# Second layers of two feed-forward blocks as three fp16 products, their inputs split by POOL and VectorE

## The chip, the cores and the metric

One core of a Trainium2 chip runs the whole program in one launch. The metric is the device time of the kernel in microseconds (us), the median of several executions. PE is TensorE, DVE is VectorE, ACT is ScalarE, POOL is GpSimd, SP is the queue that issues the DMAs.

## What is computed

32 independent batch items of 256 tokens by 256 features go through four stages. The two marked lines are what the change is about; the rest sets the work around them.

```
# per item: x is (256, 256), all in float32
x = x + W_out(silu(scale * LN2(W_in(silu(scale * LN1(x) + shift))) + shift))   # stage 0, norm over all 65536 values
x = ada(LN(x))                                                            # stage 1
x = x + Wo(softmax(q k^T / 4 + bias, masked) v)                           # 16 heads, bias (16, 256, 256) an item
x = x + gelu2(LN(x) @ W1 + b1) @ W2 + b2         # <- W1 (256, 1024), W2 (1024, 256)
x = max(x + dt * stencil(x), 0)                                           # stage 2
y = x + Wo3(causal attention(LN(x)))                                      # stage 3
y = y + gelu(LN(y) @ W3 + b3) @ W4 + b4          # <- W3 (256, 1024), W4 (1024, 256)
out = x + gate * (y - x)
```

## The kernel before

An item's activations are tiles of 128 partitions by 512 columns (two blocks of 256). All five instruction streams are written out by one loop over ticks: `begin(layer, b)` is 64 b for the first block of work (stages 0, 1 and 2) and 64 b + 160 for the last (stage 3), and the table `P` (with `OWN` for the first two and last two items, and `SPLIT`) gives each piece of work its tick from there. A tick is no time: it only fixes the order in which each engine's instructions stand, and each engine goes through its own list in that order, held by semaphores. So about three items are under way at once, and a piece that waits holds up all that stands behind it on its engine. Within a tick the order is that of the code: attention first, then the front, the middle, the stencil, the tail.

Attention is done in 16 units per item (8 for each block, two heads each), one every 4 ticks: scores on PE (L1538), bias and row maximum on DVE (L1010), exp on ACT (L1249), transposes on PE (L1548) and their copies from PSUM by ACT and DVE (L1254, L1017), the product with the values on PE (L1563). POOL adds the mask to the bias tile of each unit of the first block (L579), four tiles ahead at most, and makes the lower halves of q and k (L564, L567).

The feed-forward block of stage 1: `t2` transposes the normalized tile into bank `bM` (L1514), ACT writes it as fp16 to `hi(MB)` (`t2_out`, L1342), DVE writes what is missing as fp16 to `lo(MB)` (`t2_lo`, L949). `MB` is the tile `TN`, which stage 3 uses in the same way (`t4_out`, L1373). `widen` (L1447) makes the first layer in four quarters g of 256 hidden features, three fp16 products for each float32 one (upper x upper, upper x lower, lower x upper), from weights that were split into fp16 halves and scaled at the start (`WS`, from raw weights in `BB`: `split_scale`, `split_gains`, `split_rest` on DVE with L879, L888, L920, `split_high` on ACT, L1300). ACT adds the bias and writes the quarter to `AA[g]` (L1275), and four gelus turn `AA[0..3]` in place (L1351, after a table load). `narrow` (L1525) multiplies `AA[g]` with `W2` in float32 from `Wf` and sums the quarters in `bM`; `f1` adds the result to `X` (L1116), and the stencil follows (L1133 on DVE, L622 to L631 on POOL). Stage 3 does the same with `BB`, `bT_` and `W4` (L1264 gelu, `out` L1192).

Around them POOL has the root of the norms (`m1_rstd`: L554 to L559), and `m1_b`, which adds the bias `b21` to `X`. DVE's `all_center` (L969) reads two tiles of SBUF. At the start PE runs matmuls with no use of their result between the steps of the conditioning (`WARM`, L1397).

## Time and profile before

| | us |
|---|---|
| median of three runs | 2604.91 (2603.47 to 2608.86) |
| the profiled execution | 2604.97 |
| its span, first to last instruction | 2603.7 |
| one period in the middle (1482.10 to 1557.67) | 75.57 |

The profile is of one execution. "Busy" is the union of an engine's instructions in time; for PE the ends are modelled, as its products are pipelined. A group's row has the engine, the line, the tiles (written <- read) with shapes, the count, the busy time and the mean duration. A float32 product on PE stands as two records. The weight loads of PE (PEld) overlap with its products. A DVE or POOL instruction's duration includes any time in which it had been started and was held.

### The profile page before, as it was taken

What the parts mean: (1) busy time and instruction counts of PE and PEld (TensorE: products, weight loads), DVE (VectorE), ACT (ScalarE), POOL (GpSimd) and SP (SyncE); (2) the same over time, 40 slices, a digit from 0 to 9 for tenths busy, and PEclk for the clock granted to TensorE, in tenths of its full rate; (3) what the DMA queues carried; (4) which work ended last, traced back from release to release, by engine and by line L of the source; (5) the groups of instructions that cost most, each with busy time, mean ns of one, the idle gap of its engine ahead of it and who ended that gap; (6) DMA issues with size and microseconds to landing.
All of it is one profiled execution on the core that took longest, in us unless ns stands there. A gap on an engine that the chain in (4) does not pass through costs nothing.

```text
span 2603.7 us, 57961 instructions
## 1 busy us (share of the span) xinstructions
PE 2470.5 (95%) x19148; PEld 2005.6 (77%) x19148; DVE 2043.6 (78%) x7387; ACT 2115.3 (81%) x4694; POOL 1536.1 (59%) x1487
## 2 busy tenths in 40 slices
PE   6878999999999999999999999999999999999987
PEld 5666778778877877887887788778878877877776
DVE  6787878788888778888787888878888888878653
ACT  2466888888898888889888888988888888888875
POOL 2566666556666656666665656666556576655421
PEclk6899999999999999999999999999999999999999
DMA  5433443333344333334443333444433344433211
GB/s 205 120 119 105 121 127 113 111 106 106 107 122 126 112 110 108 107 105 122 126 115 108 108 107 106 122 127 115 114 110 100 105 121 125 123 105 96 75 29 33
DMA packets 178537, 287.67 MB, mean 110 GB/s; under 512 B 46080, under 2 KB 99328, under 8 KB 177984
## 3 DMA queue, kind: packets, MB, share of 16 engines
q1 hardware_dynamic: 178240, 283.97, 38.5%
q8 instruction: 155, 2.54, 0.4%
q14 instruction: 142, 1.16, 0.2%
HBM read 174.64 MB, written 8.45 MB: 70 GB/s over the span
## 4 chain that ended last, share of the span: by engine, by line
PE 69%; DVE 15%; SPq 4%; ACT 4%; issue 3%; POOL 2%; DMA 2%; DVEq 0%; POOLq 0%; ACTq 0%
PE bank L1525 17%; PE bank L1447 12%; PE bank L1548 10%; PE bank L1538 6%; PE bank L1563 6%; PE bank L1507 6%; DVE PB L1010 4%; PE bank L1514 3%; SPq L496 3%; PE bank L1459 3%; PE bank L1701 2%; DVE bank L969 2%; PE bank L1436 2%; SPq L492 1%; DMA Ks<-KU 1%
## 5 line engine op out<-in xcount | busy, mean ns | idle before, releaser
L1249 ACT ACTIVATE PB<-PB,mx 128x256 f32<-128x256 f32 (+1 forms) x2048 | 831.4, 473 | 35.7 <-DVE mx L1010 34.7
L579 POOL TENSOR_TENSOR BT<-BT,MN 128x1024 f32<-128x1024 f32 x256 | 556.9, 2180 | 122.5 <-DMA BT<-in_bias 121.0
L1548 PE MATMUL bank<-ident,PB 128*128 128x128 f32 x3584 | 486.4, 274 | 11.5 <-ACT PT L1254 5.5
L1010 DVE CUSTOM_DVE_ANT_0 PB<-bank,BT 128x256 f32<-128x256 f32 x1024 | 372.0, 418 | 137.8 <-PE bank L1538 132.8
L1548 PEld LDWEIGHTS bank<-ident,PB 128*128 128x128 f32 x3584 | 421.6, 141 | 63.4 <-ACT PB L1249 10.6
L1447 PE MATMUL bank<-TN,WS_w 128*128 128x256 f16 x3072 | 378.8, 273 | 38.7 <-ACT BB L1275 19.6
L1538 PE MATMUL bank<-Ks,Qs 96*128 96x512 f32 (+1 forms) x1024 | 364.6, 430 | 25.5 <-DMA Ks<-KU 12.0
L1017 DVE COPY PT<-bank 128x512 f32<-128x512 f32 (+1 forms) x512 | 315.9, 617 | 87.5 <-PE bank L1548 85.8
L1447 PEld LDWEIGHTS bank<-TN,WS_w 128*128 128x128 f16 x3072 | 282.5, 98 | 120.1 <-ACT BB L1275 35.4
L1254 ACT ACTIVATE PT<-bank 128x512 f32<-128x512 f32 (+1 forms) x512 | 272.3, 532 | 94.9 <-PE bank L1548 90.6
L1010 DVE CUSTOM_DVE_ANT_0 PB<-bank,caus 128x128 f32<-128x128 f32 (+1 forms) x1024 | 306.6, 350 | 42.3 <-PE bank L1538 42.2
L1563 PE MATMUL bank<-PT,VW 128*32 128x256 f32 (+1 forms) x4096 | 248.2, 360 | 4.4 <-DVE CX L1027 2.4
L1525 PE MATMUL bank<-Wf,BB 128*128 128x256 f32 x1024 | 236.8, 379 | 0.8 <-ACT BB L1264 0.6
L1525 PE MATMUL bank<-Wf,AA 128*128 128x256 f32 x1024 | 236.0, 383 | 0.5 <-ACT AA L1351 0.4
L1538 PEld LDWEIGHTS bank<-Ks,Qs 96*128 96x128 f32 x1024 | 168.1, 192 | 67.7 <-DVE mx L1010 22.3
L1525 PEld LDWEIGHTS bank<-Wf,AA 128*128 128x128 f32 x1024 | 192.2, 191 | 29.5 <-issue 0.9
L1525 PEld LDWEIGHTS bank<-Wf,BB 128*128 128x128 f32 x1024 | 189.6, 190 | 25.1 <-issue 1.7
L1563 PEld LDWEIGHTS bank<-PT,VW 128*32 128x32 f32 x4096 | 107.5, 109 | 98.7 <-issue 49.0
L554 POOL TENSOR_SCALAR smm<-smm 128x2 f32<-128x2 f32 x32 | 7.2, 226 | 280.0 <-DVE smm L991 280.0
L1010 DVE DVE_READ_ACCUMULATOR2_ANT mx<- 128x1 f32 x2048 | 169.0, 83 | 0.0
L1275 ACT ACTIVATE BB<-bank,cols 128x256 f32<-128x256 f32 x256 | 107.4, 470 | 44.3 <-PE bank L1447 44.3
L1260 ACT ACTIVATE ET<-bank 128x256 f32<-128x256 f32 x256 | 97.2, 380 | 46.8 <-PE bank L1563 42.7
(285 smaller groups left out, 4735.9 us busy)
## 6 DMA issues: line engine op xcount, KB each, us to landing
BT<-in_bias SPq DMA_DIRECT2D x256, 512.0 KB, 4.3
Qs<-QH SPq DMA_DIRECT2D x512, 64.0 KB, 2.4
Ks<-KH SPq DMA_DIRECT2D x1024, 32.0 KB, 2.0
Qs<-QU SPq DMA_DIRECT2D x256, 64.0 KB, 2.4
Ks<-KU SPq DMA_DIRECT2D x512, 32.0 KB, 2.0
XT<-in_xT SPq DMA_DIRECT2D x32, 256.0 KB, 2.8
X<-in_x SPq DMA_DIRECT2D x32, 256.0 KB, 2.9
AB<-ada_rows SPq DMA_DIRECT2D x32, 256.0 KB, 3.7
```

The source lines that it names most:

```text
L579: G.op.tensor_tensor(v2(BT[k % 4]), v2(BT[k % 4]), MN[:, :].unsqueeze(1).broadcast_to([128, 2, 512]), ALU.add).then_inc(g_bt, 1)
L1010: V.op.tensor_tensor_reduce(PB[(2 * D + q) % 6][:, h * 256:h * 256 + w], bS[q][:, h * w:h * w + w], plus, -1.0, 3.0e38, ALU.add, ALU.min, ...
L1017: V.op.tensor_copy(flipped(u.D, 1)[:, 0:w], bP[1][:, 0:w]).then_inc(v_ev, 1)
L1249: S.op.activation(o, o, ACT.Exp, scale=-1.0, bias=mx[u.layer][:, c:c + 1]).then_inc(a_exp, 1)
L1254: S.op.activation(flipped(u.D, 0)[:, 0:w], bP[0][:, 0:w], ACT.Copy).then_inc(a_ev, 1)
L1275: S.op.activation(half(out, m), half(ps, m), ACT.Identity, scale=scale(m), bias=bias(m)).then_inc(sem, 1)
L1447: last = T.op.matmul(half(ps, m), w, v[:, k * 256:k * 256 + 256], start=(k == 0 and i == 0), stop=(k == 1 and i == 2))
L1507: last = T.op.matmul(half(ps, m), x[:, k * 256 + m * 128:k * 256 + m * 128 + 128], Wf[:, a + k * 256:a + k * 256 + 256], start=(k == 0), s ...
L1525: last = T.op.matmul(half(ps, q), x[:, f * 256 + q * 128:f * 256 + q * 128 + 128], Wf[:, c:c + 256], start=(g == 0 and f == 0 and q == 0), ...
L1538: T.op.matmul(bS[q][:, 0:2 * w].rearrange("p (h k) -> p h k", h=2), Qs[i][0:96, et * 256 + q * 128:et * 256 + q * 128 + 128], k2[:, :, 0:w ...
L1548: last = T.op.transpose(bP[h][:, c * 128:c * 128 + 128], PB[(2 * u.D + q) % 6][:, h * 256 + k * 128:h * 256 + k * 128 + 128], ident[:, :])
L1563: last = T.op.matmul(half(bV, J % 2)[32 * s:32 * s + 32, q:256], VW[x][:, v:v + 32], flipped(u.D - 1 + et, h)[:, k * 256:k * 256 + 256 - q ...
```

## The change

Both `narrow`s take three fp16 products in place of a float32 one. `W2` and `W4` are loaded raw into `AA` and `BB` at the start, their maxima taken on DVE (`peek`), and split into fp16 halves (`narrow_high` on ACT, `narrow_rest` on DVE); `W4` is loaded twice, since `BB` holds `W3` in between. A bound for the hidden values gives one more scale, for which `split_gains` gets 19 more small operations in each block. In every item POOL writes the scaled upper half of each hidden quarter (`hidden_high`), and DVE the lower half in place (`hidden_rest`). The upper halves go to `TN` for g = 0 and 1 and to the free half of `AA[g-2]` or `BB[g-2]` for g = 2 and 3. `f1` and `out` undo the scale in the same instruction as their addition. All ticks are new: `w1_gelu` and `w2` from 64 and 68 to 62 and 70, `w3_gelu` and `w4` from 66 and 69 to 66 and 75, `f1` from 74 to 71.

```diff
+NARROW = {"w1": "w2", "w3": "w4"}
+HIDDEN = 32768.0
...
 WARM = {
-    "start": 24, "c1": 12, "n1_ones_0": 2, "v1": 9, "win_1": 5, "w1_0": 3, "n2_ones_2": 1, "n1_ones_3": 4,
-    "v1_3": 1, "v3": 10,
+    "start": 14, "c1": 13, "wout": 17, "v1": 11, "v3": 13,
...
+        def spare(x, b, g):
+            if x == 3 and b == NB - 1:
+                return (hi, lo)[g % 2](AA[g // 2])
+            return (hi, lo)[g](TN) if g < 2 else lo((AA if x == 1 else BB)[g - 2])
...
+                for b in at(t, "ld_w1"):
+                    if b == 0:
+                        S.wait_ge(p_set, 5)
+                        raw("w1", BB, d_ws)
+                        raw("w2", AA, d_wn)
...
+            def hidden_high(x, layer, b, g, sem):
+
+                G.op.tensor_scalar(spare(layer, b, g), x[:, :], narrow_scale("w2" if layer == 1 else "w4", 7), None,
+                                   ALU.mult).then_inc(sem, 1)
...
+                for b, g in steps(t, "h1_hi", 4, 1):
+                    G.wait_ge(a_h1, 4 * b + g + 1)
+                    G.wait_ge(v_ws, made("p3"))
+                    if g < 2:
+                        G.wait_ge(p_w1, 4 * b + 4)
+                    else:
+                        G.wait_ge(v_h1, 4 * b + g - 1)
+                    hidden_high(AA[g], 1, b, g, g_h1)
...
+            def peek(n):
+
+                for c in range(4):
+                    V.op.tensor_reduce(aq[:, c:c + 1], raw_narrow(n)[c][:, :], AX.X, ALU.max,
+                                       apply_absolute_value=True).then_inc(v_ws, 1)
+
+            def narrow_rest(n):
+
+                j = ("w2", "w4").index(n)
+                for c in range(4):
+                    z = 512 * c
+                    V.wait_ge(a_wn, 4 * j + c + 1)
+                    V.op.scalar_tensor_tensor(out=WS[n][:, 2048 + z:2560 + z], in0=raw_narrow(n)[c][:, :],
+                                              scalar=narrow_scale(n, 6), in1=WS[n][:, z:z + 512], op0=ALU.mult,
+                                              op1=ALU.subtract).then_inc(v_wn, 1)
...
+            def hidden_rest(x, layer, b, g, sem):
+
+                V.op.scalar_tensor_tensor(out=hi(x), in0=x[:, :], scalar=narrow_scale("w2" if layer == 1 else "w4", 7),
+                                          in1=spare(layer, b, g), op0=ALU.mult, op1=ALU.subtract).then_inc(sem, 1)
...
+                for b, g in steps(t, "h1_lo", 4, 1):
+                    V.wait_ge(g_h1, 4 * b + g + 1)
+                    hidden_rest(AA[g], 1, b, g, v_h1)
...
                     V.wait_ge(p_w2, 4 * b + 4)
                     V.wait_ge(g_m1, 5 * b + 5)
-                    V.op.tensor_tensor(x[:, :], bM[:, :], x[:, :], ALU.add).then_inc(v_f1, 1)
+                    V.op.scalar_tensor_tensor(out=x[:, :], in0=bM[:, :], scalar=narrow_scale("w2", 4), in1=x[:, :], op0=ALU.mult,
+                                              op1=ALU.add).then_inc(v_f1, 1)
...
                 for b in at(t, "t2_out"):
                     S.wait_ge(p_t2, b + 1)
-                    S.wait_ge(p_w3, 4 * (b - 2))
+                    S.wait_ge(p_w2, 4 * b)
+                    S.wait_ge(p_w4, 4 * (b - 2))
...
                 for b in at(t, "t4_out"):
                     S.wait_ge(p_t4, b + 1)
-                    S.wait_ge(p_w1, 4 * min(b + 3, NB))
+                    S.wait_ge(p_w2, 4 * min(b + 3, NB))
+                    S.wait_ge(p_w4, 4 * b)
...
-            def narrow(ps, x, w, g):
+            def narrow(ps, n, h, l, g):
                 for f in range(2):
                     for q in range(2):
-                        c = w * 2048 + (2 * g + f) * 256
-                        last = T.op.matmul(half(ps, q), x[:, f * 256 + q * 128:f * 256 + q * 128 + 128], Wf[:, c:c + 256],
-                                           start=(g == 0 and f == 0 and q == 0), stop=(g == 3 and f == 1),
-                                           skip_group_check=True)
+                        z, c = (2 * g + f) * 256, slice(f * 256 + q * 128, f * 256 + q * 128 + 128)
+                        wh, wl = WS[n][:, z:z + 256], WS[n][:, 2048 + z:2304 + z]
+                        for i, (v, w) in enumerate(((h, wh), (h, wl), (l, wh))):
+                            last = T.op.matmul(half(ps, q), v[:, c], w, start=(g == 0 and f == 0 and q == 0 and i == 0),
+                                               stop=(g == 3 and f == 1 and i == 2), skip_group_check=True)
...
                 for b, g in steps(t, "w2", 4, 1):
-                    T.wait_ge(d_w2, 16)
+                    T.wait_ge(v_wn, 4)
                     T.wait_ge(a_w1, 8 * b + 8)
-                    T.wait_ge(a_h1, 4 * b + g + 1)
-                    narrow(bM, AA[g], 0, g).then_inc(p_w2, 1)
+                    T.wait_ge(g_h1, 4 * b + g + 1)
+                    T.wait_ge(v_h1, 4 * b + g + 1)
+                    narrow(bM, "w2", spare(1, b, g), hi(AA[g]), g).then_inc(p_w2, 1)
```

Stage 3 has the same steps as `h3_hi`, `h3_lo` and `w4`, with `BB` for `AA`.

## Rows read from the trace of the kernel before

**Rows 1.** The page of before: its span, busy shares by engine, and PE's 40 slices.

```profile
span 2603.7 us, 57961 instructions
...
PE 2470.5 (95%) x19148; PEld 2005.6 (77%) x19148; DVE 2043.6 (78%) x7387; ACT 2115.3 (81%) x4694; POOL 1536.1 (59%) x1487
...
PE   6878999999999999999999999999999999999987
```

**Rows 2.** Table of stretches: us, then busy us (instructions) of each engine, PE's clock, DMA.

```profile
...
0.00:320.00 320.00, 258.57 (x1741) 204.43 (x1742) 244.40 (x799) 179.39 (x386) 171.94 (x162) 0.87 0.44 135
320.00:2240.00 1920.00, 1886.18 (x14886) 1539.63 (x14889) 1564.18 (x5707) 1660.09 (x3695) 1202.98 (x1164) 1.00 0.40 113
2240.00:2604.00 364.00, 325.74 (x2526) 261.56 (x2524) 235.03 (x883) 275.78 (x615) 161.23 (x162) 1.00 0.29 76
1482.10:1557.67 75.57, 74.37 (x590) 60.75 (x589) 61.66 (x228) 65.56 (x147) 47.95 (x47) 1.00 0.41 115
```

**Rows 3.** Groups of instructions on PE by form: shapes, count, busy us, mean ns, idle before.

```profile
...
L1447 PE MATMUL bank<-TN,WS_w 128*128 128x256 f16 x3072 | 378.8, 273 | 38.7 <-ACT BB L1275 19.6 <-ACT AA L1275 10.6 <-DVE TN L949 4.6
...
L1525 PE MATMUL bank<-Wf,BB 128*128 128x256 f32 x1024 | 236.8, 379 | 0.8 <-ACT BB L1264 0.6
L1525 PE MATMUL bank<-Wf,AA 128*128 128x256 f32 x1024 | 236.0, 383 | 0.5 <-ACT AA L1351 0.4
...
L1459 PE MATMUL bank<-WS_p,HB 128*128 128x256 f16 x384 | 48.0, 275 | 0.1
```

**Rows 4.** Timeline of the last 16 us: start, length, engine, line, count; PE's rows.

```profile
...
2587.75 5.40 PE L1447 MATMUL bank<-TN,WS_w 128*128 128x256 f16 x48
...
2592.99 7.07 PE L1525 MATMUL bank<-Wf,BB 128*128 128x256 f32 x32
```

**Rows 5.** Single lines: count, least/median/most ns, first and last start; L920's group has its mean.

```profile
L1116 DVE TENSOR_TENSOR X<-bank,X x32: 678/681/692, 158.5 to 2500.8; 128x512 f32<-128x512 f32 x32
...
L920 DVE SCALAR_TENSOR_TENSOR WS_w<-BB,ws,WS_w x8: 740/1271/2619, 76.2 to 187.0; 128x512 f16<-128x512 f32 x8
...
L1133 DVE TENSOR_TENSOR bank<-X,cB x32: 706/1404/1801, 159.7 to 2504.7; 128x512 f32<-128x512 f32 x32
...
L969 DVE SCALAR_TENSOR_TENSOR bank<-XT,sm,gT x64: 749/1759/2723, 19.0 to 2363.0; 128x512 f32<-128x512 f32 x64
...
L879 DVE TENSOR_REDUCE am<-BB x14: 407/664/681, 49.0 to 148.1; 128x1 f32<-128x512 f32 x8, 128x1 f32<-128x256 f32 x6
...
L888 DVE TENSOR_REDUCE am<-am x3: 157/157/158, 52.0 to 150.7; 128x1 f32<-128x4 f32 x2, 128x1 f32<-128x6 f32 x1
...
L920 DVE SCALAR_TENSOR_TENSOR WS_w<-BB,ws,WS_w 128x512 f16<-128x512 f32 x8 | 11.6, 1512 | 0.4 <-ACT WS_w L1300 0.4
```

**Rows 6.** Single lines of POOL: count, least/median/most ns, first and last start.

```profile
L564 POOL TENSOR_TENSOR QU<-QU,QH x64: 1267/1278/1586, 61.7 to 2536.6; 128x512 fp32r<-128x512 f32 x64
...
L573 POOL TENSOR_SCALAR MN<-MU x32: 1493/1494/1819, 73.2 to 2365.6; 128x512 bf16<-128x512 uint8 x32
...
L579 POOL TENSOR_TENSOR BT<-BT,MN x256: 2117/2138/2670, 74.8 to 2437.8; 128x1024 f32<-128x1024 f32 x128
```

**Rows 7.** Waits of DVE, then of POOL: us in total, times, longest.

```profile
...
DVE PB L1010 <- PE bank L1538: 175.0, 136, 4.3
...
POOL smm L554 <- DVE smm L991: 280.0, 32, 10.0
```

**Rows 8.** Timeline around one period: f1 and t4_out, then out.

```profile
1505.54 0.68 DVE L1116 TENSOR_TENSOR X<-bank,X 128x512 f32<-128x512 f32 x1
...
1521.11 0.60 ACT L1373 ACTIVATE TN<-bank 128x512 f16<-128x512 f32 x1 [0.23 <-PE bank L1514]
...
1544.63 0.70 DVE L1192 TENSOR_TENSOR bank<-bank,Y 128x512 f32<-128x512 f32 x1 [1.05 <-PE bank L1525]
```

**Rows 9.** Timeline of the last 16 us, ACT's first and last gelu.

```profile
...
2590.13 0.72 ACT L1264 ACTIVATE BB<-BB,ws 128x512 f32<-128x512 f32 x1
...
2594.58 0.72 ACT L1264 ACTIVATE BB<-BB,ws 128x512 f32<-128x512 f32 x1
```

More of the change, by code:

```diff
@@ L79 @@
     "v3_out", "c3", "c3_out", "o3", "m4", "m4_rstd", "m4_norm", "m4_b", "t4",
-    "t4_out", "w3", "w3_out", "w3_gelu", "w4", "out", "st_out",
[1 row of a table added]
 }
@@ L641, in gpsimd @@
                     token_rstd(smt, g_t, 6 * b, NORM)
+                for b, g in steps(t, "h3_hi", 4, 1):
+                    G.wait_ge(a_ge, 4 * b + g + 1)
+                    G.wait_ge(v_ws, made("w3") + 40)
+                    if b == NB - 1:
+                        G.wait_ge(v_s, 17 * NB)
+                    elif g < 2:
+                        G.wait_ge(p_w3, 4 * b + 4)
+                    else:
+                        G.wait_ge(v_h3, 4 * b + g - 1)
+                    hidden_high(BB[g], 3, b, g, g_h3)
                 for b in at(t, "m4_b"):
@@ new lines, in split_gains @@
+                high, wide_raw, bias, beta, wide_max, bound, up, down = (narrow_scale(NARROW[n], i) for i in (0, 1, 2, 3, 4, 5, 6, 7))
+                a = 8 * ("w1", "w3").index(n)
+                V.op.tensor_scalar(wn[:, a:a + 5], ps[:, 128:133], 128.0, None, ALU.mult).then_inc(v_ws, 1)
+                V.wait_ge(v_ws, v0 + 6)
+                V.op.tensor_tensor(bound, wide_raw, beta, ALU.mult).then_inc(v_ws, 1)
+                V.op.reciprocal(up, high).then_inc(v_ws, 1)
+                V.wait_ge(v_ws, v0 + 8)
@@ new lines, in split_gains @@
+                V.op.tensor_tensor(bound, bound, wide_max, ALU.add).then_inc(v_ws, 1)
+                V.op.tensor_scalar(up, up, LARGE, None, ALU.mult).then_inc(v_ws, 1)
+                V.wait_ge(v_ws, v0 + 10)
+                V.op.scalar_tensor_tensor(out=bound, in0=bound, scalar=256.0, in1=bias, op0=ALU.mult, op1=ALU.add).then_inc(v_ws, 1)
+                V.wait_ge(v_ws, v0 + 11)
+                V.op.reciprocal(down, bound).then_inc(v_ws, 1)
+                V.op.tensor_tensor(wide_max, bound, high, ALU.mult).then_inc(v_ws, 1)
@@ L913, in split_rest @@
                 first = sum(len(split_of(m)[1]) for m in ORDER[:ORDER.index(n)])
-                v0 = made(n) + len(parts) + 11
+                v0 = scaled(n)
                 ps = bM if n == "w1" else bT_
@@ L1187, in tail @@
                     token_stats(y, smt, v_t, 5 * b + 1)
+                for b, g in steps(t, "h3_lo", 4, 1):
+                    V.wait_ge(g_h3, 4 * b + g + 1)
+                    hidden_rest(BB[g], 3, b, g, v_h3)
                 for b in at(t, "out"):
@@ L1219, in vector @@
                         first_rest()
+                for b in at(t, "split_peek"):
+                    if b == 0:
+                        V.wait_ge(d_wn, 128)
+                        peek("w4")
+                for n in NARROW.values():
+                    for b in at(t, f"split_{n}_lo"):
+                        if b == 0:
+                            narrow_rest(n)
                 for n in ORDER:
@@ L1292, in project, with narrow_high @@
                         S.op.activation(f32r(hi), U[:, :], ACT.Copy).then_inc(a, 1)
+            def narrow_high(n):
+                S.wait_ge(v_ws, scaled("w1" if n == "w2" else "w3"))
+                if n == "w4":
+                    S.wait_ge(d_wn, 192)
+                for c in range(4):
+                    S.op.activation(WS[n][:, 512 * c:512 * c + 512], raw_narrow(n)[c][:, :], ACT.Identity,
+                                    scale=narrow_scale(n, 6)).then_inc(a_wn, 1)
             def split_high(n):
-                k0 = made(n) + len(split_of(n)[1]) + 11
+                k0 = scaled(n)
                 S.wait_ge(v_ws, k0)
@@ L1747, in tensor @@
                         T.wait_ge(v_o, 2 * b)
-                    T.wait_ge(d_w4, 16)
-                    T.wait_ge(a_ge, 4 * b + g + 1)
-                    narrow(bT_, BB[g], 1, g).then_inc(p_w4, 1)
+                    T.wait_ge(v_wn, 8)
+                    T.wait_ge(g_h3, 4 * b + g + 1)
+                    T.wait_ge(v_h3, 4 * b + g + 1)
+                    narrow(bT_, "w4", spare(3, b, g), hi(BB[g]), g).then_inc(p_w4, 1)
         loads()
```

175 lines of the change are left out of this document (118 added, 57 removed), and 148 rows, old and new, of tables (LATE, OWN, P).

## The prediction

> **What bounds the kernel now.** I read the page's shares and its slices first [rows 1]: TensorE (PE) is busy 95% of a span of 2603.7 us, and all its slices in the middle are full at full clock, while VectorE (DVE) stands at 78%, ScalarE (ACT) at 81% and POOL at 59%. The table of stretches [rows 2] shows where the rest lies. From 320 to 2240 us PE is busy 1886.2 of 1920 (98.2%); in the first 320 us only 258.6, and in the last 364 us 325.7, for there the chains of single batch items, not the amount of work, set the pace. One period, from the first layer's `t2_out` of one item at 1482.10 to the next one's at 1557.67, is 75.57 us. In it PE is busy 74.37, DVE 61.66, ACT 65.56, POOL 47.95. So in the middle the bound is PE's work, with 1.2 us of waits per item. DVE's own largest wait is for PE's scores, 175.0 us in all [rows 7]; it has 13.9 us of slack per item, POOL has 27.6. The middle holds 1920 / 75.57 = 25.4 of the 32 items; 6.6 items' worth lies in the ends.
>
> **What leaves PE.** `narrow` (L1525) is the second layer of both blocks. It runs in fp32, in which each product leaves two records; 1024 records for each block, 236.0 and 236.8 us busy [rows 3]. After the change each product is three fp16 ones: 2 blocks x 32 items x 4 quarters x 4 products x 3 = 3072, each 128x128 against 256 columns. This form is in the trace: L1447, 3072 records in 378.8 us; and L1459, where the weights are the moving side as they will be here, 384 in 48.0 us, so 125 ns each [rows 3]. By busy time the trade is 472.8 - 384 = 89 us. Busy spans of small groups overlap their neighbours', so I prefer distances between starts. In the tail 48 fp16 products start at 2587.75 and what follows starts at 2592.99: 5.24 us, 1.31 for the 12 that will make a quarter. The 32 fp32 records then run 7.07 us, 1.77 for the 8 that make a quarter now [rows 4]. The saving is 0.45 us a quarter, 3.6 us an item, 115 us in all (bounds 89 to 115). I take 0.45. With the same 1.2 us of waits PE's period would be 75.57 - 3.6 = 71.97 us. The startup's warm matmuls change a little (68 instead of 71): nothing.
>
> **What DVE gets.** Eight `hidden_rest` per item, SCALAR_TENSOR_TENSOR over 128x512, both tensor inputs in SBUF, fp16 out (256 in all). The same form stands in the trace as L920 (the weights' lower halves): least 740, median 1271, most 2619 ns; its mean, 1512, has the startup's few in it [rows 5]. The least is what the work takes; DVE ops of the same size with one input in PSUM hold 678 to 692 (L1116) and never more. The others with two inputs in SBUF stretch: L1133 706 to 1801, median 1404, where POOL runs its `s_pm`, and L969 749 to 2723, median 1759 [rows 5]. So the surplus is a wait inside the instruction while POOL is in one of its own (1.28 us for 512 elements, 2.14 for a mask addition [rows 6]). The Trainium skill, "SBUF — State Buffer", section "SBUF: two separate sides", gives the cause: a DVE instruction with two SBUF inputs and a POOL instruction exclude each other for their whole length. By that rule these 256 belong to the stretching kind, and the trace agrees (the page names no cost; the medians above do). What matters is how often POOL is in an instruction when a `hidden_rest` comes up. `hidden_high(g+1)` stands in POOL's order right behind `hidden_high(g)`, whose end releases `hidden_rest(g)`: a clash is built in for g = 0 and 2. For g of 2 and 3 POOL itself waits for `hidden_rest(g-2)`, which keeps it quiet at other moments. About half blocked: I take L920's median, 1.27 us; bounds 0.74 and 1.76. DVE per item: 61.66 + 8 x 1.27 = 71.8 us (67.6 to 75.7). `f1` and `out` stay single instructions with one input in PSUM: nothing.
>
> So DVE comes level with PE. DVE can't be busy all the time: it takes turns with PE through the same banks (scores, transposes). PE alone runs now at 98.4%; two engines that are both nearly full wait for each other more. I give DVE 97.5% at best: 71.8 / 0.975 = 73.6 us a period, against PE's 71.97. 73.6 is the forecast for the middle: 1.97 us an item less, 25.4 items: -50 us. The bounds: with unblocked halves DVE needs 67.6 / 0.975 = 69.3, PE decides, 3.6 us an item: -91. With 1.76 us each: 75.7 / 0.975 = 77.6, +2.0 an item: +52.
>
> **What POOL gets.** Eight `hidden_high` per item, TENSOR_SCALAR 128x512, fp32 to fp16. Nearest rows: 1.28 us for a two-input addition of that size, 1.49 for a TENSOR_SCALAR from uint8 [rows 6]. I take 1.28: 47.95 + 10.2 = 58.2 of 73.6 us, 79%; up to 3 us more where DVE holds it off. It doesn't bound, and costs nothing by itself. The Trainium skill, "GPSIMD Engine Reference", section 3, puts a tight one-input loop over 512 elements at 769 ns; by it POOL would need 6.2 us an item, block DVE for less, and the forecast would go toward the lower bound; no row here shows such an instruction. The first half waits for ACT's gelu, and behind it in POOL's order stand mask additions, `m1_b` and the stencil's first products. POOL now sits waiting for DVE 280.0 us in `m1_rstd` alone [rows 7], 8.75 an item, and four bias tiles lie between a mask addition and its user, so this is covered; were it not, the scores' biasing on DVE would be late by up to one chain of four gelus of 0.72 us [rows 9], 2.9 us in each block.
>
> **The longer way from gelu to the second layer.** Now `w2` starts behind the gelu; the change puts at least 1.28 + 0.74 us between, for four quarters up to 8.1. PE has other items' work in between if the order allows (the ticks part `w1_gelu` and `w2` by 8 instead of 4, 9 us), so I cost it at nothing. Uncovered it would be 2 to 8 us in each block.
>
> **TN is held longer.** TN holds the first layer's input halves, then the hidden halves of quarters 0 and 1, for both blocks in turn. Now from `t2_out` at 1482.10, where the period of [rows 2] begins, to `f1` at 1505.54, when `w2` is over, are 23.4 us, and from `t4_out` at 1521.11 to `out` at 1544.63, when `w4` is over, 23.5 [rows 8]. The free parts are 15.6 and 13.0 us. Even 8.1 us more in each leaves 7.5 and 4.9. The new waits of `t2_out` and `t4_out` for `p_w2`, `p_w4` are covered.
>
> **Start.** Raw `w2` is loaded with `w1`; DVE gets four reductions of 0.66 us (L879), some 19 small operations of about 0.16 (L888), and four lower halves of 0.74 to 1.5: 9 to 12 us [rows 5]; ACT gets four copies, and has room. Part of it lies in the first item's chain, where PE is idle anyway. The same for `w4` one item later. I take +5; bounds 0 and +20.
>
> **The ends.** Outside the middle 6.6 items' work shrinks by 3.6 us each, 24 us, but PE isn't the limit there: I take half, -12 (bounds 0, -24). The very end: the last gelu starts at 2594.58 and the fp32 products then run to 2600.06 [rows 4, 9]; new, gelu's end at 2595.30 + 1.28 + 0.74 + 1.31 is 2598.6, or 2600.3 if the four quarters' halves alternate (from the first gelu's end at 2590.85, 8.1 + 1.31): 0.
>
> **Sum**, against the profiled execution (2604.97 us with a span of 2603.7; the median of the three runs is 2604.91, the same): 2604.97 - 50 - 12 + 5 = 2548 us.
>
> **Rivals.** (a) PE stays the bound, the halves slip in unblocked, 2604.97 - 91 - 24 + 5 = 2495. For it: POOL idles 27.6 us an item, and quiet stretches of 4 to 10 us could be met. Against: the built-in clash. (b) DVE becomes the bound for worse than PE was, slower than before. From a mean `hidden_rest` of (75.57 x 0.975 - 61.66) / 8 = 1.50 us on; L920's mean of 1.51 is there already, L969's median gives 2604.97 + 52 + 10 = 2667; at 1.65 us each the period is 76.8, +30 us, about 2640. Against: a late DVE meets a POOL that waits for it. (c) Level: period 75.0 to 75.6, the gain eaten by waits between PE and DVE, or by the gelu chain; 2590 to 2610. (d) The change doesn't do what it says: fp16 products cost more here, since each brings a weight load of its own. L1447 and L1459 load as often, at 123 to 125 ns [rows 3], so I give this almost nothing; the price is 89 instead of 115 us, 7 us later in a PE-bound case.
>
> **How the numbers follow.** The forecast, 2525 to 2580, has 0.48; between it and (a) 0.17, near (a) 0.05; (c) 0.12; a small gain from 2580 to 2595 0.06; (b) 0.12. The range 2495 to 2612 leaves out (b) and a little of (a), and takes the bounds of the unknown stretch of `hidden_rest` nearly whole. 0.2% is 5 us, about what a measurement can tell from no change. Faster by more than that: 0.79; within: 0.06; slower: 0.15.
>
> **What would show it.** Right: L1525's records are 3072 fp16 of some 125 ns; the period in the middle about 73.6; DVE busy over 90% in the middle, PE below 97% there, with waits for DVE that rows of before don't have; `hidden_rest` with a least of 0.74 and a median near 1.27. Wrong: a median at 0.74 to 0.9 (then (a)); PE waiting for `hidden_rest` itself (the gelu chain isn't covered); waits of `t2_out` or `t4_out` (TN); a startup later by over 10 us at the first `f1`.

## The result, and the profile after

The changed kernel takes 2837.07 us (median of 4 runs, 2832.17 to 2837.49), the kernel before 2605.12 beside it: ratio 1.0884, 95% interval 1.0868 to 1.0900. It is slower by 232 us; the prediction said 57 us faster. The page of the changed kernel, its first part and two of its slices' rows, against [rows 1]:

```profile
span 2835.9 us, 60959 instructions
## 1 busy us (share of the span) xinstructions
PE 2456.8 (87%) x20148; PEld 1928.3 (68%) x20148; DVE 2352.1 (83%) x7689; ACT 2114.6 (75%) x4702; POOL 1981.1 (70%) x1743
...
PE   6677888988898898888888988888998889988887
...
PEclk7879999999999999999999999999999999999999
```

No engine is full any more. Most of PE's slices of 9 have become 8s, and it is not the clock that took them away: the granted clock is still 9 (tenths of full speed) in every slice from the fourth on, and 0.99 on average in the middle. The stretches, columns as in [rows 2]:

```profile
320.00:2240.00 1920.00, 1710.84 (x14408) 1350.61 (x14407) 1649.96 (x5417) 1519.54 (x3395) 1436.59 (x1255) 0.99 0.36 104
```

PE is busy 89% of the middle (98.2% in [rows 2]), DVE 86%, ACT 79%, POOL 75%. The period comes most exactly from `f1`, one instruction an item (name, form, count, ns least/median/greatest, first and last start):

```profile
L1244 DVE SCALAR_TENSOR_TENSOR X<-bank,wn,X x32: 743/747/752, 172.2 to 2729.1; 128x512 f32<-128x512 f32 x32
```

(2729.1 - 172.2) / 31 = 82.48 us. Before, the same instruction (L1116) started at 158.5 first and at 2500.8 last: 75.56 us. All periods below are worked out so. The whole loss can be placed with it: the first `f1` is 13.7 us later, 31 periods are 6.92 us longer each (214.6), and from the last `f1` to the span's end it is 106.8 us instead of 102.9. Sum 232.2, the difference of the two spans. The loss is in the repeated part.

What each engine is busy per item is its share of the middle times 82.48: PE 73.5, DVE 70.9, ACT 65.3, POOL 61.7. The two kinds of new instruction, DVE's `hidden_rest` and POOL's `hidden_high`, by tile (ns least/median/greatest):

```profile
L1069 DVE SCALAR_TENSOR_TENSOR AA<-AA,wn,TN x64: 743/1173/2643, 160.4 to 2722.6; 128x512 f16<-128x512 f32 x64
L1069 DVE SCALAR_TENSOR_TENSOR BB<-BB,wn,TN x62: 743/748/1181, 371.4 to 2809.8; 128x512 f16<-128x512 f32 x62
...
L593 POOL TENSOR_SCALAR TN<-AA,wn x64: 1561/1572/1860, 157.0 to 2720.9; 128x512 f16<-128x512 f32 x64
```

And waits of PE, of DVE and of POOL (engine, line waited at, releaser: us in all, times, longest). Those at L1692, L1069 and L593 are new; PE's wait for DVE's maxima was 10.6 us before, and POOL's for the bias tile 121.0:

```profile
PE bank L1704 <- DVE mx L1135: 66.2, 99, 4.2
PE bank L1692 <- DVE AA L1069: 49.3, 58, 3.7
...
DVE AA L1069 <- POOL TN L593: 83.4, 57, 2.7
...
DVE PB L1135 <- PE bank L1704: 44.3, 57, 3.6
...
POOL TN L593 <- ACT BB L1405: 167.4, 30, 29.5
POOL BT L623 <- DMA BT<-in_bias: 141.8, 36, 8.6
...
POOL TN L593 <- ACT AA L1506: 25.6, 22, 12.8
```

The new ones, read from the bottom up, are the steps of one path: gelu (ACT) to `hidden_high` (POOL) to `hidden_rest` (DVE) to the product (PE, L1692). PE and DVE wait at it for the block with `AA`; for `BB` PE's wait for the lower half is 3.6 us in all, and it is POOL that stands early, waiting for the gelu. DVE's wait for PE's scores, 175.0 us in [rows 7], has shrunk to 44.3; PE now waits for DVE's maxima, 66.2. The two changed places. How POOL's list stands in it is seen in its timeline, with ACT's gelus of the second block last (start, us, what, idle time before it and what ended it):

```profile
1510.85 1.28 POOL L689 TENSOR_TENSOR Y<-X,rows 128x512 f32<-128x512 f32 x1
1518.45 3.12 POOL L593 TENSOR_SCALAR TN<-BB,wn 128x512 f16<-128x512 f32 x2 [6.32 <-ACT BB L1405]
...
1553.13 2.13 POOL L623 TENSOR_TENSOR BT<-BT,MN 128x1024 f32<-128x1024 f32 x1 [5.04 <-DMA BT<-in_bias]
1555.28 1.57 POOL L593 TENSOR_SCALAR TN<-AA,wn 128x512 f16<-128x512 f32 x1
...
1554.46 2.56 ACT L1506 ACTIVATE AA<-AA,ws 128x512 f32<-128x512 f32 x4
```

POOL stands 6.32 us before the halves of one block, waiting for their gelu. Before the halves of the other block it stands 5.04 us for a bias tile and then adds the mask. It looks as if that made the halves late, but it did not: their first gelu started at 1554.46 and took 0.71 us, so its result was there at 1555.17, and POOL began 0.11 us later. The timeline of the whole run shows the same. In 29 of the 32 items the first half of `AA` starts within 0.2 us of the first gelu's end, and that of `BB` always. POOL begins on time; what it adds to the path is what the halves, and the small steps between them, take.

### The profile page after: what moved, and what is told of

The parts are those of the page before. It is cut to its first block, busy times and chain, and to the rows that moved or that the text cites. A ratio compares the mean times of both kernels' runs of the same rounds, so it can differ in the third digit from the quotient of the medians.

```text
span 2835.9 us, 60959 instructions
## 1 busy us (share of the span) xinstructions
PE 2456.8 (87%) x20148; PEld 1928.3 (68%) x20148; DVE 2352.1 (83%) x7689; ACT 2114.6 (75%) x4702; POOL 1981.1 (70%) x1743
## 4 chain that ended last, share of the span: by engine, by line
POOL 27%; DVE 24%; PE 22%; ACT 12%; issue 10%; SPq 2%; DMA 1%; DVEq 0%; POOLq 0%; ACTq 0%
POOL TN L593 6%; POOL BT L623 6%; PE bank L1604 6%; DVE PB L1135 5%; PE bank L1692 3%; PE bank L1714 3%; ACT PB L1390 2%; PE bank L1672 2%; ACT AA L1416 2%; PE bank L1679 2%; PE bank L1729 2%; POOL AA L593 2%; PE bank L1704 2%; DVE PT L1142 2%; DVE BB L1069 2%
## 5 line engine op out<-in xcount | busy, mean ns | idle before, releaser
L623 POOL TENSOR_TENSOR BT<-BT,MN 128x1024 f32<-128x1024 f32 x256 | 571.3, 2242 | 141.9 <-DMA BT<-in_bias 141.8
L1714 PE MATMUL bank<-ident,PB 128*128 128x128 f32 x3584 | 564.1, 277 | 17.2 <-DVE PT L1142 11.5
L1714 PEld LDWEIGHTS bank<-ident,PB 128*128 128x128 f32 x3584 | 445.5, 143 | 97.2 <-ACT PB L1390 22.1
L1704 PE MATMUL bank<-Ks,Qs 96*128 96x512 f32 (+1 forms) x1024 | 425.0, 449 | 88.8 <-DVE mx L1135 66.2
L593 POOL TENSOR_SCALAR TN<-BB,wn 128x512 f16<-128x512 f32 x62 | 96.9, 1570 | 167.4 <-ACT BB L1405 167.4
L1692 PE MATMUL bank<-WS_w,AA 128*128 128x256 f16 x1056 | 170.9, 274 | 36.3 <-DVE AA L1069 27.0
L1692 PE MATMUL bank<-WS_w,TN 128*128 128x256 f16 x1008 | 176.9, 278 | 24.9 <-DVE AA L1069 22.3
L1692 PE MATMUL bank<-WS_w,BB 128*128 128x256 f16 x1008 | 162.9, 273 | 2.8 <-DVE BB L1069 1.6
L1416 ACT ACTIVATE AA<-bank,cols 128x256 f32<-128x256 f32 x256 | 107.4, 470 | 50.3 <-PE bank L1604 49.6
L1692 PEld LDWEIGHTS bank<-WS_w,AA 128*128 128x128 f16 x1056 | 99.8, 98 | 60.8 <-issue 34.8
```

The lines of the kernel that those rows point to most:

```text
L593: G.op.tensor_scalar(spare(layer, b, g), x[:, :], narrow_scale("w2" if layer == 1 else "w4", 7), None, ALU.mult).then_inc(sem, 1)
L623: G.op.tensor_tensor(v2(BT[k % 4]), v2(BT[k % 4]), MN[:, :].unsqueeze(1).broadcast_to([128, 2, 512]), ALU.add).then_inc(g_bt, 1)
L1416: S.op.activation(half(out, m), half(ps, m), ACT.Identity, scale=scale(m), bias=bias(m)).then_inc(sem, 1)
L1692: last = T.op.matmul(half(ps, q), v[:, c], w, start=(g == 0 and f == 0 and q == 0 and i == 0), stop=(g == 3 and f == 1 and i == 2), skip_g ...
L1704: T.op.matmul(bS[q][:, 0:2 * w].rearrange("p (h k) -> p h k", h=2), Qs[i][0:96, et * 256 + q * 128:et * 256 + q * 128 + 128], k2[:, :, 0:w ...
L1714: last = T.op.transpose(bP[h][:, c * 128:c * 128 + 128], PB[(2 * u.D + q) % 6][:, h * 256 + k * 128:h * 256 + k * 128 + 128], ident[:, :])
```

## The experiments

Five parts of the change can be had one by one: the start, the shorter products, the new order, the hand-overs of the halves, and the time that the halves take. The first four runs (a single execution each; the kernel before gave 2602.84 on the same chip) keep the new order and take parts of the halves away.

**New order, fp32 products, no halves.** The `hidden_high` and `hidden_rest` steps are gone, and the products are the old ones; they read columns of `Wf` that hold other weights, in the same form and number.

```diff
-                        for i, (v, w) in enumerate(((h, wh), (h, wl), (l, wh))):
-                            last = T.op.matmul(half(ps, q), v[:, c], w, ...
+                        last = T.op.matmul(half(ps, q), h[:, f * 256 + q * 128:f * 256 + q * 128 + 128], Wf[:, z:z + 256],
```

> The changed kernel with all its new ticks and its startup, but the second layers in float32 as before (from tiles AA and BB, against float32 weights of another layer, so the values differ) and no hidden halves on POOL and DVE. It is the old work in the new order. If the new order costs the time (theory ORDER), at least 2750 us. If the halves cost it (theories POOL or DVE), within 2600 to 2640: the startup's 14 us and little else.

2781.61 us, period 80.63. The new order and the new start, with the work of before in the middle, cost 5.1 us an item. This was the first sign of the step that failed.

**New order, fp16 products, no halves.** The products take weight tiles as operands.

```diff
-                    narrow(bM, "w2", spare(1, b, g), hi(AA[g]), g).then_inc(p_w2, 1)
+                    narrow(bM, "w2", WS["w2"][:, 0:512], WS["w2"][:, 512:1024], g).then_inc(p_w2, 1)
```

> The changed kernel without the hidden halves on POOL and DVE; the fp16 products read weights in their place and wait for the gelus alone. It shows what PE's saving is worth where nothing is added: by my forecast's term 3.6 us an item less than the run in float32 where PE bounds (about -115 us against it); theory ORDER: as slow as the float32 one, since PE isn't the bound there.

2672.25 us, period 77.2: the shorter products give 109 us, 3.4 us an item (forecast: 3.6 and 115). In this order the saving comes through nearly whole.

**One half at a time.** First POOL's halves whole and DVE's of 2 columns; then DVE's whole and POOL's of 2 columns. The products read weight tiles where a half is missing.

```diff
-                V.op.scalar_tensor_tensor(out=hi(x), in0=x[:, :], ...
+                V.op.scalar_tensor_tensor(out=hi(x)[:, 0:2], in0=x[:, 0:2], ...
```

> POOL makes the whole upper halves, DVE only two columns of each lower half; PE reads weights as the lower halves. All waits stand. Theory POOL (the halves stand in the middle of POOL's order and hold up what is behind them): at least 2780 us. Theory DVE (1.17 us instructions with the lock take DVE's slack): 2650 us or less.

```diff
-                G.op.tensor_scalar(spare(layer, b, g), x[:, :], ...
+                G.op.tensor_scalar(spare(layer, b, g)[:, 0:2], x[:, 0:2], ...
```

> The other way round: POOL writes two columns of each upper half, DVE the whole lower halves; all waits stand. Theory DVE: at least 2780 us. Theory POOL: 2650 us or less. If both single ones lie near 2740, each adds its part to one common chain.

2782.07 and 2786.54 us. Either half alone costs 110 to 114 us over the run without halves, both together 165. The price of POOL's part, which the forecast put at nothing, is as large as that of DVE's. Two loads on two independent bounds would leave the larger one; two links of one chain would add up. They seem to lie between, but both runs contain all the hand-overs, and a later run prices these.

**The old order with room for the halves.** The obvious question is whether the old ticks would have been better. They can't be kept as they are, since TensorE would wait at `w2` for halves that come later in the lists of engines that wait for TensorE. So `w2` goes from 68 to 70, `w4` from 69 to 73, `out` from 74 to 76, `st_out` from 71 to 73. The rest stays, but for a few ticks of the start and of the first and last two items.

```diff
-    "w2": 68, "w4": 69, "out": 74, "st_out": 71,
+    "w2": 70, "w4": 73, "out": 76, "st_out": 73, "h1_hi": 58, "h1_lo": 66, "h3_hi": 54, "h3_lo": 70,
```

> The whole change (fp16 products, both halves, the new startup) with the old kernel's ticks for all that existed before; the new pieces are put in by hand (POOL's upper halves at 58 and 54, DVE's lower halves at 66 and 70, w2 at 70, w4 at 73, out at 76, and a few ticks of the last two items). My forecast of 2548 us was for a kernel with the old order's waits. Theory ORDER AND HALVES (the new order costs 5 us an item by itself, the halves 5 more, whatever the order): 2837 - 179 = about 2660 us. If my sum was right and only the order was missed: 2530 to 2580. If the halves need the new order: above 2700.

3649.39 us, ratio 1.4004 (1.3975 to 1.4034). The same ticks with fp16 products and no halves, with POOL's halves alone and with DVE's alone:

> The fp16 products in the old order, without the hidden halves (weights are read in their place): PE's saving in the order in which PE was the bound. By the forecast's term 3.6 us an item: 75.6 - 3.6 = 72.0 us a period, 2604.97 - 115 + 5 = about 2495 us. If the saving is as in the new order (109 us), the same within 10.

> As old_order, but DVE writes only two columns of each lower half and PE reads weights for them: POOL's share of the cost in the old order. Theory POOL: as slow as old_order within 30 us. Theory DVE: near old_f16_none.

> As old_order, but POOL writes only two columns of each upper half (DVE subtracts weights in their place, and PE reads the same weights): DVE's share in the old order. Theory DVE: as slow as old_order within 30 us. Theory POOL: near old_f16_none. If both are slow, the chain gelu, POOL, DVE, PE and its waits cost, not the work of one engine.

2908.56, 3572.7 and 3513.08 us, a single execution each. `old_f16_none` missed its expectation by over 400 us, and `old_high_only` both of its cases (it lies 77 us below `old_order`). For `old_order` and `old_rest_only` only the last case of each held, that the halves need the new order and that the chain costs and not the work of one engine; neither had named a price near the 900 to 1040 us above the kernel before. Waits of `old_order`, the whole change in this order, for PE, DVE and POOL, and its middle stretch:

```profile
PE bank L1574 <- POOL X L544: 247.4, 29, 10.6
PE bank L1587 <- DVE AA L964: 213.7, 30, 9.7
...
DVE AA L964 <- POOL TN L488: 256.2, 37, 15.6
...
POOL AA L569 <- DVE X L1139: 259.3, 31, 13.5
...
320.00:2240.00 1920.00, 1413.09 (x10804) 1089.07 (x10802) 1197.16 (x4052) 1151.54 (x2544) 1069.10 (x942) 0.85 0.27 78
```

I read them as a ring: PE waits at `w2` (L1587) for DVE's half, DVE for POOL's half, POOL in the stencil for DVE's `f1` (L1139), which needs `w2`, and the next block's halves stand behind that in POOL's list. Each of these waits is 7 to 8.4 us an item, the period is 107.6, and no engine is over 74% busy. For the halves the new order is thus 812 us better than this one, and it is no waste by itself. But even the run without halves, at 2908.56, is 303 us slower than the kernel before, from which it differs in a few ticks, the shorter products and the start. Hence the next runs.

**Moved ticks by themselves.** The kernel before, complete, with only these ticks later (and `w2` of the first and last two items by one or two):

```diff
-    "w2": 68, "w4": 69, "out": 74, "st_out": 71,
+    "w2": 70, "w4": 73, "out": 76, "st_out": 73,
```

> The kernel before, complete and with fp32 second layers; only the ticks of w2 (68 to 70), w4 (69 to 73), out (74 to 76) and st_out (71 to 73) are later. Theory that a piece moved by a few ticks in TensorE's list is what costs: 2800 to 3000. Rival, that the cost comes with the shortened fp16 products or the reordered start: 2600 to 2640, as before.

2947.78 us, ratio 1.1323 (1.1302 to 1.1345), period 86.3: the theory holds. Moving a few matmuls that PE has to do anyway two to four ticks back costs more than the change under study. DVE's `f1` and `out` in that run, each with its idle time:

```profile
L1021 DVE TENSOR_TENSOR X<-bank,X x32: 685/692/693, 157.0 to 2833.5; 128x512 f32<-128x512 f32 x32
its engine sat idle before it (us, times) until:
  PE bank L1430: 129.6, 30
...
L1097 DVE TENSOR_TENSOR bank<-bank,Y x32: 689/700/700, 347.6 to 2939.2; 128x512 f32<-128x512 f32 x32
its engine sat idle before it (us, times) until:
  PE bank L1430: 129.1, 31
```

In the kernel before the same instruction idled once:

```profile
L1116 DVE TENSOR_TENSOR X<-bank,X x32: 678/681/692, 158.5 to 2500.8; 128x512 f32<-128x512 f32 x32
its engine sat idle before it (us, times) until:
  PE bank L1525: 1.0, 1
```

Now DVE stands 8.3 us an item with the scores of the next heads behind it, and PE needs those. Two runs ask how this price behaves. One tick instead of two to four:

```diff
-    "w2": 68, "w4": 69, "out": 74, "st_out": 71,
+    "w2": 69, "w4": 70, "out": 75, "st_out": 72,
```

> The kernel before, complete, with the second layers and what reads them one tick later: w2 68 to 69, w4 69 to 70, out 74 to 75, st_out 71 to 72; f1 stays at 74. A tick is 75.6/64 = 1.2 us here. Moved by two and four ticks, f1 and out stood 8.6 us an item for TensorE and the period rose by 10.8 us. If the price begins where the slack between w2 and f1 (six ticks, 7 us) is used up: 2610 to 2680. If any move costs as much as the large one, because the neighbours in TensorE's list change: 2850 to 2950. No price: 2600 to 2610.

2675.83 us, ratio 1.0272 (1.0249 to 1.0295), period 77.7, 32.3 us of standing at `f1`. It begins at the first tick, with +71 us (68 against the kernel before on the same chip), and grows with the distance. PE's wait for ACT's copy of the transposed probabilities is 31.5 us there, 5.5 in the kernel before, and for DVE's maxima 31.3 against 10.6. And the readers moved along, so that `f1` and `out` stand as far behind the products as in the kernel before (the edit is against the run with ticks moved by two to four):

```diff
-    "f1": 74, "s_r": 75, "out": 76, "st_out": 73,
+    "f1": 76, "s_r": 77, "out": 78, "st_out": 75,
```

> The kernel before with w2, w4 and out late as in the run that moved these alone (86.3 us a period), and now f1 (74 to 76), s_r and a further two ticks of out (to 78) and st_out (to 75) later as well. In that run VectorE stood 4.3 us an item at f1 and 4.3 us at out, behind TensorE. If those 8.6 us of standing were the price of the move, most of the 343 us goes: 2620 to 2720. If the price lies in TensorE's own list: 2850 to 2950.

3050.2 us, ratio 1.1708, period 89.7. Neither expectation has it: it grew by 102 us, though the standing at `f1` is gone:

```profile
L1021 DVE TENSOR_TENSOR X<-bank,X x32: 678/685/691, 163.8 to 2944.3; 128x512 f32<-128x512 f32 x32
its engine sat idle before it (us, times) until:
  PE bank L1430: 6.4, 3
...
DVE PB L915 <- PE bank L1443: 303.2, 136, 10.4
...
POOL AA L527 <- DVE X L1021: 220.8, 31, 8.8
```

The wait went to others: POOL's stencil now stands 220.8 us for `f1` (140.6 with only the products moved, 21.2 in the kernel before), DVE 303.2 for scores (192.7, and 175.0 in [rows 7]). Part of the price is not waiting at all. PE's busy time an item is 74.2 us in the kernel before, 77.0 with the products moved and 78.7 here, for the same matmuls, at a granted clock of 1.00, 0.98 and 0.95 in the middle. So my account of that price by DVE's standing alone is refuted; which of PE's neighbours costs what in these lists stays open.

**The old order to the tick.** Without halves the old ticks can be kept, all but those of the loads and the new steps of the start and four of the last two items. Two runs, first with fp16 products on weight tiles, then with the fp32 products of the first experiment; both with the change's start.

```diff
-    "w1_gelu": 62, "w2": 70, "f1": 71, "w4": 75, "out": 76, ...
+    "w1_gelu": 64, "w2": 68, "f1": 74, "w4": 69, "out": 74, ...
```

> Leaves out: both halves of the hidden values (the three fp16 products read weight tiles in their place), so the output is not the reference's. The order is the old one to the tick: w2 at 68, w4 at 69, out at 74. If the saving on TensorE is real and only the order stood in its way, the time falls by the term of the forecast, 89 to 115 us and some us of start: 2490 to 2530. If moving w2 and w4 by two to four ticks was not what made the run with shifted ticks 300 us slower, it stays near that one, 2850 to 2910.

> Complete, second layers in fp32 and no halves, the old order to the tick; what is left of the change is its start (the narrow weights' halves are made before the first items). It prices the start by itself. The run with fp16 products in this order was 2584 with the first f1 at 179.8 us against 158.5 before. Expected: the period of before, 75.6 us, and a start 15 to 25 us longer, 2618 to 2632; so that TensorE's shorter products gave 35 to 45 us in this order. Rival, a start that is covered later: 2600 to 2610.

2584.45 us (ratio 0.9924, 0.9909 to 0.9939) and 2639.64 (1.0129, 1.0107 to 1.0151). Each lies above its expected range, the first by 54 us, the second by 8. The second is not complete, contrary to its expectation, but reads other columns of `Wf`, like the first experiment. Periods 74.23 and 75.90. The start and what comes with it cost 33 us against the kernel before on the same chip: the first `f1` is at 173.8 us instead of 158.5 (15), 31 periods are 0.34 us longer each (11), and from the last `f1` to the end it is 7 us more. The shorter products give 55 us here, 1.67 an item, not the 3.6 of the forecast. The middles of the fp32 and of the fp16 run:

```profile
320.00:2240.00 1920.00, 1886.07 (x14894) 1536.96 (x14893) 1566.12 (x5710) 1659.43 (x3698) 1209.42 (x1166) 1.00 0.39 113
...
320.00:2240.00 1920.00, 1851.94 (x16064) 1499.60 (x16062) 1599.72 (x5839) 1694.14 (x3783) 1230.73 (x1191) 1.00 0.40 116
```

PE's busy time an item falls from 74.6 (1886.07 / 1920 x 75.90) to 71.6 us, but its gaps grow from 1.3 to 2.6. They lie in the attention: PE's wait for ACT's copy of the transposed probabilities is 30.4 us in all (5.5 in the kernel before), for DVE's maxima 21.9 (10.6). My reading, which no run tests, is that scores, bias and maximum, exponential, transposes and copies go round PE, DVE and ACT, and that `w2` and `w4` were filler that gave the other two time.

**More work off PE, no halves.** If fewer products are the point, the halves can be dropped: the gelu writes fp16, and two products remain (hidden values rounded to fp16, which the change avoids).

```diff
-                        for i, (v, w) in enumerate(((h, wh), (h, wl), (l, wh))):
+                        for i, (v, w) in enumerate(((h, wh), (h, wl))):
...
-                S.op.activation(BB[g][:, :], BB[g][:, :], ACT.Gelu, scale=scale_of("w3", 0)).then_inc(a_ge, 1)
+                S.op.activation(hi(BB[g]), BB[g][:, :], ACT.Gelu, scale=scale_of("w3", 0)).then_inc(a_ge, 1)
```

> Old order to the tick. The gelu writes its result as fp16 at once and the second layers are two fp16 products (hidden times high half, hidden times low half of the weight); POOL and VectorE make no halves. The hidden values are then rounded to fp16, which the kernel of the change does not do. Each quarter has 12 fp16 matmuls where the three products have 18 records' worth, so TensorE loses a further 0.4 us a quarter, 3 us an item. If the order lets the saving through: 2400 to 2460. If ScalarE (65.6 us of each 75.6 before) or another chain takes over early: 2460 to 2520. If TensorE is no longer the bound after the first 115 us, it equals the run with three products and no halves.

2596.21 us, ratio 0.9963 (0.9950 to 0.9975). This beats both kernels, by 9 us over the one before. But it has a third fewer fp16 products in the second layers than the fp16 run above and is 12 us slower. Of its expectation only the third case is near, that it equals that run. Its middle and PE's wait, from an execution of 2603.27 us, 7 above the median:

```profile
320.00:2240.00 1920.00, 1797.26 (x15138) 1423.49 (x15137) 1595.02 (x5801) 1684.89 (x3754) 1221.92 (x1183) 0.98 0.40 114
...
PE bank L1609 <- ACT PT L1290: 80.2, 35, 2.8
```

Period 74.68, PE busy 69.9 of it: 1.7 us less an item, and 2.1 us more gaps. The products taken away are worth more than 1.7 us. All second-layer products were busy 366.8 us in the run above and are 255.7 here, 3.5 us an item less. About half of that is eaten up inside PE's busy time, at a granted clock of 0.98 in the middle where the run above has 1.00: the transposes (280 ns in the mean against 275) and the products with the values (406 against 390) are longer. How much of the 12 us is the clock and how much the attention's waits no run separates. What is shown is that beyond the first 1.7 us of shorter period, work taken off PE bought nothing in this order.

**What of the halves costs.** The changed kernel with all its waits and signals, the halves of 2 columns on both engines, the products on weight tiles:

```diff
-                G.op.tensor_scalar(spare(layer, b, g), x[:, :], ...
+                G.op.tensor_scalar(spare(layer, b, g)[:, 0:2], x[:, 0:2], ...
...
-                V.op.scalar_tensor_tensor(out=hi(x), in0=x[:, :], ...
+                V.op.scalar_tensor_tensor(out=hi(x)[:, 0:2], in0=x[:, 0:2], ...
```

> Leaves out: POOL's and VectorE's instructions for the halves write 2 columns in place of 512, and the fp16 products read weight tiles; all waits and signals of the changed kernel stay, and so does its order. Without the halves this order gave a period of 77.2 us, with them 82.5. If it is their duration (1.57 us on POOL, 1.0 to 1.6 us on VectorE, 8 of each an item) that costs: 2675 to 2720. If it is the hand-overs gelu to POOL to VectorE to TensorE in queues that are worked in order: 2760 to 2837.

2709.12 us, ratio 1.0397 (1.0374 to 1.0420), period 78.5. The hand-overs cost 37 us (1.3 an item over 77.2), the duration of the halves 128 us (4.0 an item). That the hand-overs in ordered queues are the larger part is refuted, the more so as the short instructions are not free: POOL's take 0.29 us each, DVE's 0.48 in the mean. With these 37 us taken off, POOL's halves alone cost 73 us and DVE's alone 77. Their sum, 150, is not far above the 128 of both together: what the two engines spend on the halves nearly adds up, as in a chain.

**The mask addition.** In the changed kernel POOL's `mask_add` 4 ticks later, so that the halves don't stand behind it:

```diff
-    "mask_add": -25,
+    "mask_add": -21,
```

> The changed kernel, complete; only POOL's addition of the mask comes 4 ticks later (-25 to -21), so that fewer halves queue behind it while it waits for its bias tile (141.8 us of waiting, 36 times). If POOL's standing in front of the halves is on the chain that sets the period: 2740 to 2815. If not: 2825 to 2850. Worse than 2850 if the bias then comes late for the scores.

2923.77 us, ratio 1.1215 (1.1188 to 1.1243), period 85.2: the run went the third way that the expectation named. POOL's waiting for the bias tile fell from 141.8 to 24.9 us, and in its place came

```profile
DVE PB L1115 <- POOL BT L603: 75.9, 34, 4.1
...
POOL TN L573 <- ACT AA L1486: 174.6, 29, 12.8
```

DVE now stands for the masked bias (5.1 us before the move), and POOL waits for the gelu of `AA` instead of the bias tile (25.6 us before). The path through the halves gains nothing: PE waits 48.7 us for `hidden_rest` of `AA` (49.3 before), DVE 82.1 for POOL (83.4). That agrees with the timeline above, in which POOL wasn't late for the gelu.

## Why the prediction was wrong, step by step

The loss adds up over a row of runs, each a step from the one before it: start and the rest of the new frame +35 us (2604.9 to 2639.6), shorter products in the old order -55 (to 2584.5), the new order +88 (to 2672.3), hand-overs +37 (to 2709.1), duration of the halves +128 (to 2837.1). Sum +232. The run at 2672.3 is a single execution, and the runs stand on several chips, on which the kernel before had medians of 2602.8 to 2607.8. The division between the steps depends on their sequence: in the new order the shorter products give 109 and the order by itself costs 142 (2639.6 to 2781.6). The forecast failed at two terms that it put at nothing, the new order (88 to 142 us) and the way through the halves (37 + 128 = 165 us), and in one that it took whole, PE's saving (55 us came through in the old order, not 115).

- **The new ticks.** This is the step that failed first. The text has the ticks only as cover for the gelu's path, and gives their replacement no term and no rival. They cost 88 to 142 us at equal work. The trace of before had a sign: DVE's `f1` waited 1.0 us in all, with `w2` six ticks ahead of it. A table so exactly used up is itself a resource, and the change has to move `w2` away from `w1_gelu`. Which of the new ticks cost the 88 to 142 us is not shown: nearly all differ, and the runs that move single ones start from the old table.
- **"In the middle the bound is PE's work".** True as a reading, 98.2%, but wrong as the derivative. Of 3.0 us that leave PE in the old order 1.67 reach the period. The forecast took 1.2 us of waits as fixed; they doubled. This is what rival (c) says, a gain eaten by waits between PE and DVE or by the gelu chain; it has the right mechanism, but its 2590 to 2610 us is far short of 2837.
- **DVE.** The load was right: 70.9 us an item against 71.8. `hidden_rest` has a mean of 1.19 us (305.0 us in 256) against 1.27 taken, least 0.72 to 0.74, and stretches to 2.64 where POOL works beside it. But 97.5% as DVE's ceiling was not what held: it is 86% busy. Rival (b) has the right sign and the wrong mechanism; it asks for DVE at its ceiling. (Its sum 2604.97 + 52 + 10 = 2667 has 10 us for start and ends where the forecast has 5 and -12; the text doesn't say from where.)
- **POOL "doesn't bound, and costs nothing by itself".** `hidden_high` took 1.57 us, above the 1.28 taken and the 1.49 of the other row that the text names, and its half alone cost 110 us, 73 without the hand-overs. Its share of 75% says nothing about a link in a chain: 8 x 1.57 = 12.6 us an item lie between gelu and product. The Trainium skill, "GPSIMD Engine Reference", section 3, has 769 ns for a tight loop over 512 elements. The rows here show about twice that, 1.57 us; the measurement decides.
- **The longer way from gelu to the second layer,** put at 0, "uncovered it would be 2 to 8 us in each block". It was uncovered: PE waits 49.3 us for the `hidden_rest` of `AA` itself (1.5 us an item), and DVE 83.4 us for POOL's half (2.6). The text had named this as a mark of being wrong. It gave 2 to 8 us in each block, 4 to 16 an item; the halves with their hand-overs cost 5.3 us an item (82.48 - 77.20), inside that. The choice of 0 was the mistake.
- **PE's saving** was right in size: 3072 fp16 records, and 3.4 us an item where it came through. **TN** was right: no large wait of ACT stands for it (2.8 and 2.3 us in all).
- **Start** +5, bounds 0 and +20: the first `f1` came 13.7 us later, inside, though past the 10 us that the text names as a sign of being wrong. The whole new frame, with its small share in each period and at the end, cost 33 us in the old order, outside. **Ends** -12: measured +3.9 after the last `f1`, outside the bounds of that term.

## What to carry to other kernels

A share of 98% tells which engine to relieve, not what the relief is worth: ask what the second engine on the same loop does with less time, and expect the gain to stop early (here 1.7 of 3.0 us). In a kernel whose engines work hand-made lists in order, a changed order is a term of the sum: find the instructions that wait almost nothing for a producer placed closely ahead, and price every producer that the change has to push back. A new stage between two others costs its duration along the chain even on an engine that is a quarter idle and begins it on time. Before a wait in a timeline is blamed, look at when what stands behind it could have started.

## What the runs showed of the hardware

POOL's multiplication with a column from fp32 to fp16 over 128x512 took 1557 ns at the least and 1562 to 1572 in the median of each tile, in 256 executions, longer than its two-input addition of the same size (1.28 us).

`hidden_rest` stretched from 0.72 to 2.64 us. How it is held shows in the run with 2 columns on both engines. On the last two quarters of `AA` the 2-column instruction takes 1235 ns in the median, on the first two 218:

```profile
L1069 DVE SCALAR_TENSOR_TENSOR AA<-AA,wn,TN x64: 202/218/243, 161.4 to 2597.5; 128x2 f16<-128x2 f32 x64
L1069 DVE SCALAR_TENSOR_TENSOR AA<-AA,wn x64: 208/1235/2176, 162.4 to 2598.2; 128x2 f16<-128x2 f32 x64
...
1490.95 1.49 DVE L1069 SCALAR_TENSOR_TENSOR AA<-AA,wn 128x2 f16<-128x2 f32 x1
...
1490.29 2.13 POOL L623 TENSOR_TENSOR BT<-BT,MN 128x1024 f32<-128x1024 f32 x1
```

The instruction of DVE starts inside POOL's mask addition and ends 0.02 us after it, at 1492.44: what it takes is the rest of POOL's instruction, not its own work. The next one, at 1494.13, takes 1.23 us and ends 0.02 us after the POOL addition that was running then. POOL's halves can't be what holds it there, at 0.29 us each. In the whole kernel it is similar. With POOL's halves alone cut to 2 columns the mean of `hidden_rest` stayed: on `AA` 1.29 us against 1.32 (165.1 and 169.4 us in 128 each), on `BB` 1.04 against 1.06 (132.7 and 135.6 in 128 each), while the median on `AA` fell from 1173 to 773 ns. So the clash that the prediction saw built in between `hidden_high` and `hidden_rest` is not what sets the mean; with POOL's halves short, its other work, such as the mask addition above, holds DVE for as long. The clash exists all the same: with POOL's halves whole and DVE's of 2 columns, DVE's took 181.2 us in all, against 123.5 with both short.

In `old_order` PE was busy 74% of the middle, and its granted clock there was 0.85 on average, between its levels of 1.2 and 2.4 GHz; in the old order with fp16 products and no halves, at 96% busy, it was 1.00. PE's busy time an item was 79.2 us (1413.09 / 1920 x 107.6) in the one and 71.6 in the other, with the same matmuls: 7.6 us more. Not all of it is the clock: in the changed kernel, at a clock of 0.99 and with gaps, it was 73.5. I put the other 5.7 us to the lower clock. That the gaps in PE's list brought the clock down fits these rows, but no run separates the two.
